# Who computes four lower weight pieces in the last two attention steps: VectorE or GpSimd

## The reference, cut to what matters

```
x = layernorm(x + conv(x) * x)                      # recurrence over the 32 items
q, k, v = relu(x@Wq+bq), relu(ctx@Wk+bk), relu(ctx@Wv+bv)
x = layernorm(x + (ln_g * norm(softmax(q k^T / 4) v + q) + ln_b))
xn = rms_norm(x) * scale;  id = argmin_e |xn - centroid[e]|^2
a, g = split(xn @ up_w[id]);  x = layernorm(x + (a * silu(g)) @ down_w[id])
```

## Time and profile before

| | us |
|---|---|
| median of 3 runs | 1162.03 |
| lowest and highest | 1159.24, 1162.17 |
| profiled execution, its own time | 1161.1 |
| its span in the trace | 1159.3 |
| step 30, about | 691 to 716 |
| step 31, about | 716 to 741 |
| drain, about | 741 to 765 |

### The profile page before, as it was taken

The page is one execution under the profiler, slowest core; times in us unless marked ns, Lnnn a source line. Parts: engine busy times, 40 slices in busy tenths (PEclk is TensorE's granted clock), DMA queues, the critical chain, the costliest instruction groups (busy, mean ns, idle before and its releaser), DMA issues.

```text
span 1159.3 us, 27851 instructions
## 1 busy us (share of the span) xinstructions
PE 1106.3 (95%) x8314; PEld 822.3 (71%) x8315; DVE 915.7 (79%) x2437; ACT 665.2 (57%) x1417; POOL 769.4 (66%) x933
## 2 busy tenths in 40 slices
PE   4999999999999999999999999989999999999995
PEld 3776666666667667667667666668788888888884
DVE  5669999999999999999999998987655555555553
ACT  4277777777777777777777777643222232322221
POOL 4748899999989989989989963345333333333333
PEclk9999999999999999999999999979999999999998
DMA  5867776776776776766775764024644444454542
GB/s 141 187 137 151 163 170 150 163 169 145 167 162 154 167 161 157 165 165 152 167 168 141 150 122 83 11 64 147 182 139 153 140 157 154 145 155 143 157 147 86
DMA packets 129473, 169.14 MB, mean 146 GB/s; under 512 B 14502, under 2 KB 116527, under 8 KB 124752
## 3 DMA queue, kind: packets, MB, share of 16 engines
q1 hardware_dynamic: 122832, 150.74, 53.4%
q0 software_dynamic: 6528, 16.99, 5.0%
HBM read 111.36 MB, written 44.11 MB: 134 GB/s over the span
## 4 chain that ended last, share of the span: by engine, by line
PE 80%; DVE 12%; issue 3%; ACT 2%; SPq 1%; DMA 1%; POOL 0%; POOLq 0%; DVEq 0%; ACTq 0%
PE S L1241 11%; PE M L1198 11%; PE Y L489 10%; PE O L1190 9%; PE G L451 8%; PE A L451 8%; PE T L1254 4%; DVE neg_max_sb L1568 3%; PE M L1261 3%; PE M L1170 3%; DVE o L1773 3%; PE GT L461 3%; PE M L1217 2%; PE M L1269 2%; PE M L1177 2%
## 5 line engine op out<-in xcount | busy, mean ns | idle before, releaser
L1568 DVE TENSOR_REDUCE neg_max_sb<-S 128x2 f32<-128x512 f32 x512 | 327.0, 680 | 48.3 <-PE S L1241 46.6
L1030 ACT ACTIVATE probs<-T 128x512 f32<-128x512 f32 x512 | 277.3, 596 | 86.9 <-PE T L1254 75.3
L1241 PE MATMUL S<-k_st,q_st 48*128 48x256 f32 x1024 | 204.2, 310 | 10.4 <-DVE neg_max_sb L1568 9.7
L1254 PE MATMUL T<-q_st,k_st 49*128 49x256 f32 x1024 | 203.3, 311 | 2.6 <-ACT probs L1030 1.5
L1241 PEld LDWEIGHTS S<-k_st,q_st 48*128 48x128 f32 x1024 | 140.0, 185 | 71.2 <-issue 53.9
L429 ACT ACTIVATE gT<-GT 128x512 f32<-128x512 f32 x71 | 42.5, 598 | 207.6 <-PE GT L461 207.6
L1254 PEld LDWEIGHTS T<-q_st,k_st 49*128 49x128 f32 x1024 | 141.1, 186 | 15.7 <-ACT probs L1030 12.8
L409 POOL DMA_INDIRECT out<-res,token x71 | 76.0, 1070 | 102.0 <-DVE res L576 97.0
L1190 PE MATMUL O<-probs,v_aug 128*32 128x256 f32 x2048 | 140.5, 393 | 0.8 <-ACT probs L1030 0.7
L489 PE MATMUL Y<-dn_sb,gT 128*128 128x256 f32 x568 | 134.5, 379 | 2.4 <-DMA dn_sb<-in_L_ffn_down_w 1.6
L489 PEld LDWEIGHTS Y<-dn_sb,gT 128*128 128x128 f32 x568 | 107.2, 189 | 21.1 <-DMA dn_sb<-in_L_ffn_down_w 3.9
(11 more groups left out here) (212 smaller groups left out, 2557.5 us busy)
## 6 DMA issues: line engine op xcount, KB each, us to landing
dn_sb<-in_L_ffn_down_w SPq DMA_DIRECT2D x71, 512.0 KB, 3.8
k_st<-k_pieces SPq DMA_DIRECT2D x64, 256.0 KB, 5.1
xr<-buckets SPq DMA_DIRECT2D x71, 129.0 KB, 2.1
xt<-in_x SPq DMA_DIRECT2D x32, 256.0 KB, 5.9
ct<-in_ctx SPq DMA_DIRECT2D x32, 256.0 KB, 6.2
k_pieces<-k_hi SPq DMA_DIRECT2D x32, 256.0 KB, 4.5
k_pieces<-k_lo SPq DMA_DIRECT2D x32, 256.0 KB, 3.0
k_st<-k_pieces SPq DMA_DIRECT2D x64, 128.0 KB, 4.4
```

The costliest lines, as they stand in the source:

```text
L1030: a_.activation(probs[:, h % 8].rearrange("p k t -> p (k t)"), T_ps[h % 2][:, :], ACT.Exp, scale=DH ** -0.5).then_inc(s["exp_ok"], 1)
L1241: last = t_.matmul(S_ps[h % 2][:, c * TOK:(c + 1) * TOK], q_st[h // HPC][base:base + STACK, h % HPC, c * P:(c + 1) * P], k_st[h // HPC][ba ...
L1254: last = t_.matmul(T_ps[h % 2][:, c * TOK:(c + 1) * TOK], k_st[h // HPC][base:base + AUG, h % HPC, c * P:(c + 1) * P], q_st[h // HPC][base ...
L1568: v.tensor_reduce(neg_max[:, cur.mod(2), :, h], S_ps[h % 2][:, :].rearrange("p (c t) -> p c t", c=NTC), AX.X, ALU.max, negate=True).then_i ...
```

## The change

Pieces 0 and 1 (step 30) and 4 and 2 (step 31) move from VectorE to GpSimd. There both of a step are issued one behind the other, right behind `offset`. Piece 3 stays on VectorE at the same place, and so do 5, 6 and 7. The counts of filler products fall from 3 to 2 at six places of step 30, and in step 31 from 5 to 4 at four places and from 7 to 4 at two. The expert phase waits for 4 of the pieces on each of two semaphores in place of 8 on one.

```diff
-LO_AT = {(SEQ - 2, 3): (0,), (SEQ - 2, 10): (1,), (SEQ - 1, 3): (4,), (SEQ - 1, 8): (2,), (SEQ - 1, 13): (3,)}
+LO_AT = {(SEQ - 1, 13): (3,)}
+LO_ON_POOL = {SEQ - 2: (0, 1), SEQ - 1: (4, 2)}
@@ expert phase, tensor @@
-                        pe.wait_ge(z["lo_dve"], E)
+                        pe.wait_ge(z["lo_dve"], E - 4)
+                        pe.wait_ge(z["lo_pool"], 4)
@@ gpsimd @@
+                def lower(e):
+
+                    pool.wait_ge(z["up_hi"], PIECES.index(e) + 1)
+                    at = slice(e * UPW, (e + 1) * UPW)
+                    g.tensor_tensor(up_sb[:, at], up_sb[:, at].bitcast(F32), up_hi[:, at].bitcast(F32), ALU.subtract).then_inc(z["lo_pool"], 1)
+
                     offset(b)
+                    for e in LO_ON_POOL.get(t.k, ()):
+                        lower(e)
                     conv_real(t + 3)
@@ tensor, step @@
-                            keep_busy(3 if t.k == SEQ - 2 else 5 if h < 12 else 7, M_ps[1])
+                            keep_busy(2 if t.k == SEQ - 2 else 4, M_ps[1])
```

More of the change, by code:

```diff
@@ L223, in build @@
         up_hi = sb2("up_hi", [P, E * UPW], F32R)
-        names2 = """dn0 dn1 table_pool early table tails up_hi lo_dve tile0 tile1 tile2 tile3 xs_ok xsT_pe xsT_hi xsT_lo
+        names2 = """dn0 dn1 table_pool early table tails up_hi lo_dve lo_pool tile0 tile1 tile2 tile3 xs_ok xsT_pe xsT_hi xsT_lo
             g_pe a_pe gate_ok gated_ok gT_pe gT_ok y_pe y2_ok ln3 rstd3 res_ok token_ok sent0 sent1 pool_waits sp_waits dve_waits"""
```

## The result

| | before | after |
|---|---|---|
| median, us | 1162.03 | 1167.03 |
| lowest and highest | 1159.24, 1162.87 | 1166.25, 1169.07 |
| profiled execution, its span | 1159.3 | 1166.9 |

Each kernel ran five times. The ratio is 1.0048, 95% interval 1.0037 to 1.0059: the change makes the kernel 0.5% slower. The forecast was 1169.8 us, the range 1164.0 to 1173.0.

What follows compares the result with a forecast made beforehand. TensorE and VectorE were taken to bound steps 30 and 31 by turns; stalls behind GpSimd's pieces, net of filler and subtraction gains, add 8.7 us to the profiled 1161.1, giving 1169.8 us, range 1164.0 to 1173.0.

Steps and rivals of the forecast that it cites:

- The exclusion: VectorE instructions with two inputs outside PSUM and GpSimd instructions exclude each other throughout; a moved piece takes 4.7 us.
- The place: Behind `offset`: VectorE meets the first piece at L1791 (L1801 after) every time, standing 3.3 us in step 30.
- Who goes next: Step 30: L1766 goes next after L1791, 0.65 us, then piece 1 until 712.1, with L1795 standing behind it.
- Scores of head 10: Step 30: TensorE's scores wait for the bank of head 8, starting at 712.9 in place of 708.55, 4.35 us late.
- Start of step 31: Step 31 starts 5.2 us late, or 3.5 without the half clock behind step 30's stall.
- Head 10 of step 31: Its scores wait for the maximum of head 8, starting at 742.0 in place of 733.25, 8.75 us late.
- Leaving the steps: End of step 31: small gains and some 1.7 us of new half clock leave it 8.6 to 8.8 us late.
- The filler's gain: Steps 30 and 31: 16 filler products fewer at 0.22 us each, 3.5 us at most.
- The expert phase: Behind the two steps: its new wait is met 20 us earlier; no term in the sum.
- VectorE gets in three times: Rival: L1795 also goes ahead of piece 1, and the one-hot row meets it; +3.5 us, 1164.6; chance 0.13.
- The pieces run beside VectorE: Rival: long GpSimd pieces give the port up in between, or L1791 comes after both; -5 to -7 us, 1156; chance 0.06.
- The half clock stays: Rival: TensorE keeps the lower clock 3.4 us longer in each step or the drain; +12 us, 1173; chance 0.11.

Runs made afterwards that it cites:

- no input: Kernel after, each GpSimd subtraction replaced by two memsets of zeros that read nothing, so four lower pieces aren't made; ratio 0.9932 to before.
- old filler: Kernel after, pieces still on GpSimd, with the filler counts of before (3; 5 and 7); ratio 1.0092 to before.
- filler in the stall: Kernel after, with 18 filler products in place of 2 or 4 ahead of head 10's scores in both steps; ratio 1.0058 to before.
- less filler alone: Kernel before, all pieces on VectorE, with only the filler counts cut (3 to 2; 5 and 7 to 4); ratio 0.9999 to before.
- after again: Kernel after, unchanged, measured again on the chip of three other runs; 1169.93 us against 1163.19, ratio 1.0055.
- both spread kernels: Kernel after with GpSimd pieces in quarters spread behind short GpSimd steps: all four pieces, 1.0001; only 0 and 4, with 1 and 2 on VectorE, 1.0005 of before.
- one piece a step: Kernel after with only pieces 0 and 4 on GpSimd, 1 and 2 back on VectorE at their old places; ratio 1.0003 to before.
- pieces left out: Kernel after without the four GpSimd subtractions and the wait for them, so four lower pieces aren't made; ratio 0.9931 to before.

## Why the prediction was right, and where it was not

The forecast was +8.7 us. The profiled pair gives +8.0 (1169.07 against 1161.1), the medians +5.0, the ratio +5.6. By its steps:

- **The exclusion** was right, in kind and length. It holds for an instruction of 4.54 us, where the trace of before reached 2.36, and "no input" ties it to GpSimd's reads. The piece is 4.54 us and not 4.7, within the bounds; the two together took 9.03.
- **The place** was right: VectorE meets the piece at L1801 in both steps, with 3.10 and 2.67 us of wait (3.3 predicted).
- **Who goes next** was wrong. I let L1776 (L1766 of before) go ahead of the second piece and L1805 stand behind it. In seven of the eight collisions of after, its repeat, "old filler" and "filler in the stall" the second piece went first and L1776 stood. It changes nothing in the sum, since the maxima are behind both: 711.99 against 712.2 predicted.
- **Scores of head 10**, step 30: predicted 4.35 us late, measured 4.18, or 3.7 counted from the start of the stretch. From the start of the first piece to the maxima it took 9.50 us, where the working had 10.2.
- **Start of step 31**: 5.2 predicted, 6.60 measured, 6.1 from the start of the stretch. Here a term was mis-sized. The half clock stood at 1.8 us in the working, for 4.3 us of work; it was 10.2 us long, and "filler in the stall" puts its price at 3.3.
- **Head 10 of step 31**: 8.75 predicted, 8.92 measured, 8.4 from the start of the stretch. This is close by luck in part: `offset` ends at 731.96 and not at 731.0, and the 9.51 us from the first piece to the maxima were again shorter than in the working (10.35).
- **Leaving the steps**: 8.6 to 8.8 predicted for the whole rest; the expert phase starts 9.8 us late by the stretch. I had counted one spell of half clock behind the second stall; the trace has one from 46.8 to 53.6 and one from 60.5 to 63.9 us behind the start, and the drain has as much half clock as before (13.7 us in both).
- **The filler's gain**, 3.5 us as an upper bound and used in parts in the steps, was too large for this kernel. Measured on the stretch it is -0.3 with VectorE as the bound (less filler alone against before) and 1.1 with the stalls (old filler against after). With the pieces gone it is 1.2 to 2.4 by the stretch, and 3.6 by the medians of one chip. A product saved is worth its length at most where nothing else ends last.
- **The expert phase** I took for unchanged. From tile 0 to tile 20 it takes 111.95 us in before's trace and 109.46 in after's. All traces fall in two groups, 108.6 to 109.8 and 111.3 to 112.0, and those of the long group (before, after again, both spread kernels) are the ones that have one more spell of half clock there, of 3.4 us, some 5 us behind the first `gate`. Nothing that the change touches runs there. After again has a ratio like that of after and is in the long group, so it isn't a steady gain of the change; but one can't read the difference of two single traces as the difference of two kernels below some 2.5 us.

The stretches differ by 9.8 us and the medians by 5.0, and the record accounts for the gap to 0.2 us. The expert phase takes 2.5 back, the later start of the stretch adds 0.5, and the profiled execution of after is the slowest of its five, 2.0 above their median, while that of before lies 0.9 below its own. The trace of after again is also its slowest, 4.2 above. So the stretches of 88.81 and 90.76 are on the high side for their kernel, and the forecast lies 2.8 us above the measured median. That +8.7 came so near to the +8.0 of the profiled pair is luck in part: the stretch grew by 1.1 more than forecast, and the expert phase, which I took for unchanged, took it back. In "one piece a step" the 4.0 us of the stretch are 1.3 to tile 20, at a ratio of 1.0003.

More half clock in other executions of before is no explanation: the granted clock is 0.986 in its trace and 0.984 to 0.989 in its 46 executions on two of the chips, and 0.981 in after's trace and 0.980 to 0.982 in its five. What stays open is what sets the two groups of the expert phase, and how long the stretch is in the executions that weren't traced.

Of the rivals, "VectorE gets in three times" would have shown a short L1805 with a long one-hot row: L1805 was short, but because L1776 had stood in its place, and the one-hot row (L1811) took 0.15 us. "The pieces run beside VectorE" falls with L1801. "The half clock stays" was half right, as the spell of 10.2 us shows, but its price doesn't show at the end of the kernel.

## What to carry to other kernels

Before elementwise work is moved from VectorE to an idle GpSimd, look up the longest GpSimd instruction that reads SBUF, and ask which two-input instruction of VectorE comes next in its queue and who waits behind that: each such instruction costs VectorE up to the whole length of GpSimd's, and the latter takes twice as long as it did on VectorE (4.54 us for 2.28). Cut in quarters the harm went, but so did the gain. Idle time on an engine that shuts VectorE out while it reads is no room that can be had for free; "pieces left out" priced it at 5.1 us of the stretch, the best kernel that makes all pieces got 1.75 of it, and none showed in a ratio.

## What the runs showed of the hardware

- A GpSimd memset of 2048 f32 columns takes 1.81 us, and the steps of VectorE that ran beside it took 0.17, 0.62 and 0.17 us as usual. A subtraction of 2048 columns takes 4.54, and the two-input instructions that met it stood until it ended (L1801 3.27 us, L1776 5.00). The maxima, which read PSUM, took 0.65 to 0.72 us in all thirteen traces.
- It works the other way too: a piece of 4.54 us took 4.99, and a quarter of 1.27 us took 1.66, when a VectorE instruction had gone ahead.
- With two GpSimd subtractions queued back to back, one short VectorE instruction got done where they meet; the one right behind it lost its turn seven times of eight.
- Idle time of 3.87 us came with 10.2 us of half clock in after, longer than the 3.4 us of the earlier trace rows behind 1.03 us of idle time. The length doesn't follow the idle time: 3.71 us came with 6.8 in "old filler", 4.04 with 13.7 in after again, and 6.37 with 6.8 in step 31 of after. With TensorE kept busy by filler there was none, and VectorE's waits were the same to 0.1 us.
